# Attention on one Trainium2 core: the statistics of the next batch's first norm taken at the end of a round instead of in the first half of the following one

## What is computed

```python
x = x + 0.5 * _L0_ffn_ref(_layernorm(x), router_w, w1, w2, bias)
x = x + _L0_attn_ref(_layernorm(x), w_qkv, w_gated, w_proj, gn_weight, gn_bias)
x = x + 0.5 * _L0_ffn_ref(_layernorm(x), router_w, w1, w2, bias)

def _layernorm(x, axis=-1, eps=1e-05):
    m = jnp.mean(x, axis=axis, keepdims=True)
    v = jnp.var(x, axis=axis, keepdims=True)
    return (x - m) / jnp.sqrt(v + eps)
```

## Time and profile before

| | |
|---|---|
| median of three runs | 2312.23 us |
| time of the profiled execution | 2312.59 us |
| its span, first to last instruction | 2310.8 us |
| outside the span | 1.8 us |
| busy: TensorE, VectorE, ScalarE, GpSimd | 2170.1, 1358.5, 1003.8, 1171.7 us |
| attention stage | about 905 to 1560 us |
| rounds 0 to 7 begin at (`mask(8b, 0)` on VectorE) | 931.55, 988.41, 1055.31, 1125.64, 1201.15, 1271.39, 1342.39, 1417.02 us |

### The profile page before, as it was taken

How to read it: one execution, slowest core, us unless ns; L and a number is a source line. 1 busy time by engine, 2 the same in 40 slices (tenths; PEclk the granted TensorE clock), 3 DMA queues, 4 the chain that set the end, 5 groups by cost and what they waited for, 6 DMA issues and landing times.

```text
span 2310.8 us, 57931 instructions
## 1 busy us (share of the span) xinstructions
PE 2170.1 (94%) x22549; PEld 1907.2 (83%) x22549; DVE 1358.5 (59%) x3312; ACT 1003.8 (43%) x2149; POOL 1171.7 (51%) x911
## 2 busy tenths in 40 slices
PE   7869999999999997999999999849999999999998
PEld 6759999999999987777777777638999999999997
DVE  7755555555555552578778877645555555555553
ACT  4434434343434342446555555434344444444442
POOL 5755777735354533223344453454777654444443
PEclk9999999999999998999999999869999999999999
DMA  9523444434343424102211121123444443434432
GB/s 365 211 81 68 101 93 99 99 87 98 82 104 81 105 55 119 39 21 76 76 40 59 59 77 75 60 81 94 100 92 102 90 101 86 100 87 99 89 80 32
DMA packets 138440, 211.52 MB, mean 92 GB/s; under 512 B 34092, under 2 KB 114544, under 8 KB 132080
## 3 DMA queue, kind: packets, MB, share of 16 engines
q0 software_dynamic: 57344, 69.21, 17.9%
q1 hardware_dynamic: 80912, 139.72, 17.5%
HBM read 138.13 MB, written 72.88 MB: 91 GB/s over the span
## 4 chain that ended last, share of the span: by engine, by line
PE 52%; DVE 4%; issue 2%; ACT 1%; another core or an unknown queue 0%; POOL 0%; DMA 0%; POOLq 0%; DVEq 0%; ACTq 0%
PE bank L675 16%; PE bank L657 15%; PE bank L768 10%; PE bank L856 3%; PE bank L889 1%; PE bank L824 1%; PE bank L644 1%; PE bank L839 1%; PE bank L874 1%; PE bank L928 1%; PE bank L786 1%; DVE aw L1829 0%; DVE rt L1817 0%; DVE xnl L1803 0%
## 5 line engine op out<-in xcount | busy, mean ns | idle before, releaser
L1167 ACT ACTIVATE h<-bank 128x512 f32<-128x512 f32 x512 | 306.1, 598 | 850.9 <-PE bank L657 740.0
L1738 DVE CAST hh<-h 128x512 fp32r<-128x512 f32 x512 | 241.2, 471 | 692.6 <-ACT h L1167 578.8
L675 PE MATMUL bank<-w2h,hh 128*128 128x256 f32 x2048 | 579.1, 283 | 3.1 <-ACT yb L1185 3.1
L675 PE MATMUL bank<-w2h,hl 128*128 128x256 f32 x2048 | 573.7, 280 | 0.0
L675 PE MATMUL bank<-w2l,hh 128*128 128x256 f32 x2048 | 573.7, 280 | 0.0
L675 PEld LDWEIGHTS bank<-w2h,hh 128*128 128x128 f32 x2048 | 385.1, 188 | 45.4 <-ACT yb L1185 3.6
L675 PEld LDWEIGHTS bank<-w2h,hl 128*128 128x128 f32 x2048 | 384.8, 188 | 41.5
L675 PEld LDWEIGHTS bank<-w2l,hh 128*128 128x128 f32 x2048 | 385.2, 188 | 39.4
L657 PE MATMUL bank<-xh,w1h 128*128 128x512 f32 x1024 | 405.1, 396 | 2.0 <-issue 1.7
L657 PE MATMUL bank<-xh,w1l 128*128 128x512 f32 x1024 | 404.3, 395 | 0.0
L657 PE MATMUL bank<-xl,w1h 128*128 128x512 f32 x1024 | 404.1, 395 | 0.0
(11 more groups left out here) (215 smaller groups left out, 3305.0 us busy)
## 6 DMA issues: line engine op xcount, KB each, us to landing
stg<-in_L_ffn_w SPq DMA_DIRECT2D x64, 1024.0 KB
xb<-acc SPq DMA_DIRECT2D x9, 1024.0 KB
xa<-in_L_attn_x SPq DMA_DIRECT2D x8, 1024.0 KB, 14.4
xn_rows<-xa SPq DMA_DIRECT2D x8, 1024.0 KB
xn_rows<-xn_r SPq DMA_DIRECT2D x8, 1024.0 KB
xr<-acc SPq DMA_DIRECT2D x7, 1024.0 KB
out_rows<-xr SPq DMA_DIRECT2D x7, 1024.0 KB
slot_table<-pay,idx POOLq DMA_INDIRECT x256
```

Source lines behind the costliest of these rows:

```text
L675: product = pe.matmul(tile_sum(j, t, end), a[:, fj, t * P:(t + 1) * P], c[:, fj, :], start=(fj == 0 and i == 0 and (end or t % 2 == 0)), s ...
L1167: act.activation(h32[fj % 2][:], bank[fj % 2][:], ACT.Gelu_apprx_tanh).then_inc(f.gelu, 1)
L1738: dve.tensor_copy(hh[:, fj, :], h32[fj % 2][:]).then_inc(f.hh, 1)
```

## The change

Only the order of VectorE's list in the attention stage changes; no instruction is added or removed. In round b, the four calls `front_stats(b + 1, 0..3)` leave the first half. At the end of round b, behind `front_low(b + 1, 3)`, there are four calls `front_stats(b + 2, 0..3)`, among and behind `channel_stats(n + 6)` and `carry(n + 8, 1)`. Batch 0's statistics are taken ahead of round -1. Batch 1's are now taken at the end of round -1 and batch 7's at the end of round 5.

```diff
                 mask(n, 0)
                 channel_stats(n - 1)
-                front_stats(b + 1, 0)
                 channels(b - 1)
...
                 about_head(b - 1)
-                front_stats(b + 1, 1)
                 head_variance(b - 1)
                 mask(n + 1, 0)
                 carry(n + 1, 1)
-                front_stats(b + 1, 2)
                 rotate(n + 3)
...
                 affine(b - 1)
-                front_stats(b + 1, 3)
                 residual_choices(b - 2)
...
                 front_low(b + 1, 3)
+                front_stats(b + 2, 0)
                 channel_stats(n + 6)
+                front_stats(b + 2, 1)
                 carry(n + 8, 1)
+                front_stats(b + 2, 2)
+                front_stats(b + 2, 3)
...
             start_residual()
+            for j in range(NT // 2):
+                front_stats(0, j)
             for b in range(-1, B):
                 sequence(b)
```

## The result

Timed in turns with the kernel before, the changed kernel takes 2318.02 us (median of 19 runs, 2313.07 to 2323.24) against 2312.87 us (19 runs, 2306.39 to 2317.22): 5.15 us more, a ratio of 1.0027 with a 95% interval of 1.0019 to 1.0036. The interval lies clear of 1. The forecast was 2316.1 us, that is +3.9 us or 0.17%, and the range 2311.5 to 2320.0. The measured time lies inside the range. The difference is larger than the forecast's +3.9 us, and close to the +5.35 us of rival 1 with one stretch of low clock (2317.6 us; two would make 2319.0).

A forecast was written before the change was run, and what follows sets the result against it. TensorE, nearly full, was taken to bound the kernel, so VectorE edits count only where TensorE waits. Terms 0 + 0 + 1.9 + 2.0 = +3.9 us on 2312.2 gave 2316.1 us, range 2311.5 to 2320.0.

The forecast's parts named there:

- rival 1: TensorE's clock falls behind new idle time in rounds 0 and 1; 1.45 us per stretch, 2317.6 us with one; chance 0.27.
- First half of the rounds: Removing 2.64 us of VectorE statistics from the first half of rounds 0 to 6 gains 0.
- line 1558 was to wait about 0.1 us or less: Sign in rounds 2 to 6: VectorE's first routing step hardly waits for TensorE's turned logits.
- End of rounds 1 to 5: Added statistics fit VectorE's free 2.24 us; mask at most 0.40 us late, covered by projection products; cost 0.
- the idle time that the prediction called gone: Sign at the meetings of rounds 1 to 5: VectorE no longer idles ahead of the mask, and TensorE doesn't wait.
- End of round -1: Four statistics pairs delay `mask(0, 0)` by 2.64 us, so TensorE's `scores(0, 1)` starts late; cost 1.9 us.
- End of round 0: VectorE has no slack; later masks and line 1888 delay TensorE's `head_variances` in round 1; cost 2.0 us.
- The loads: Statistics at a round's end now need a load issued in the same round; wait costed at 0.
- The clock: The forecast's sum held no cost for a fall of TensorE's clock behind the new waits: 0.
- Rivals 2: The last statistics pair ahead of the routing gains 0.66 us in each of rounds 2 to 6; 2312.8 us; chance 0.14.
- rival 3: Costs at rounds -1 and 0 are made up later, first halves gain; about 2307.6 us or less; chance 0.05.
- rival 4: A load lands late and `front_stats(2, 0)` waits at the end of round 0; 2317.1 us; chance 0.05.

The follow-up runs named there:

- experiments 6 and 7: 6: kernel before without the statistics of batches 3 to 7, ratio 1.0004; 7: kernel before with each round's first statistics pair moved behind `about_head`, ratio 1.0002.
- late_only: Kernel before with statistics moved to the end of a round only for batches 3 to 7; ratio 0.9994.
- batch2_only: Kernel before with only batch 2's statistics moved, to the end of round 0; ratio 1.0009.
- changed_again: The changed kernel unaltered, profiled and timed a second time against the kernel before; ratio 1.0025, 2299.07 us.
- fill_waits: Changed kernel with TensorE's waits ahead of `scores(0, 1)` and round 1's `head_variances` filled by unread transposes; ratio 1.0010 against the kernel before.
- the doubled one: Changed kernel with eight more unread `bn_stats` at the ends of rounds -1 and 0 each; ratios to the kernel before 1.0058 and, repeated, 1.0059.

## Why the prediction was right and where it was short

- **First half of the rounds, taken as 0: right.** No statistics at all for batches 3 to 7 gains nothing (1.0004). For rounds 2 to 6 the reason is the one given, TensorE's turned logits and then GpSimd's step. One detail was wrong: line 1558 was to wait about 0.1 us or less in rounds 2 to 6, and it waits 0.51 us in each, as in round 7. The working had itself said that the freed time turns up there as idle time. The Trainium skill (SBUF — State Buffer, Who interferes with whom) has such steps blocked for a whole GpSimd instruction; the pairs of rows of experiments 6 and 7 agree, with common ends to within 0.1 us.
- **End of rounds 1 to 5, taken as 0: right.** The mask came 0.22 us late in `late_only` (bound 0.40) and nobody waited. In the profile of the changed kernel the mask of round 6 (at 1355.02 us) still stands idle for 0.64 us until TensorE has its scores; TensorE's clock was low just there (0.50 from 1354 on). So the idle time that the prediction called gone was not gone in every round.
- **End of round -1, taken as 1.9 us: right.** 1.87, 1.88 and 1.87 us in three kernels.
- **End of round 0, taken as 2.0 us: somewhat too much.** The net waits were 1.19 us in the profile of after, 1.44 in `batch2_only` and 1.44 in `changed_again`. `scores(8, 1)` waits 0.44 to 0.68 us, and then `head_variances` 1.21 or 1.22, of which 0.46 were there. VectorE's part was right: the first mask is 2.64 us later in its list, and the second follows 2.33 us behind it (forecast 2.25). But the wait is VectorE's lateness against TensorE, and the working took TensorE as on time. Its `scores(8, 0)`, ahead of the projection products, started at these times before and after, and the last line is VectorE's line 1888 after:

```profile
987.68 0.67 PE L856 MATMUL bank<-qm,qkT 32*64 32x128 f32 x16
...
998.81 0.67 PE L856 MATMUL bank<-qm,qkT 32*64 32x128 f32 x16
...
1007.26 0.16 DVE L1888 SCALAR_TENSOR_TENSOR gsm<-gmv,gsm 128x2 f32<-128x2 f32 x1
```

  From the first to line 1888 it is 7.20 us before and 8.45 after: 1.25 us more, where the working had 1.98. TensorE was late itself, since its clock was low just ahead: from `front_pair` (line 786) to `scores(8, 0)` it took 2.02 us before and 2.67, 2.44 and 2.62 in the three profiles. That accounts for most of what is missing. How long the waits are with a full clock ahead of round 1 was not measured.
- **The loads, taken as 0: right.** In the profile of after VectorE waits for `xb` once, for batch 0, and never again in the attention stage.
- **The clock, taken as 0 in the forecast: the term that failed.** The waits give 3.1 to 3.3 us, the median 5.15 and the repeated comparison 0.25%, 5.7 us. The remainder, 2 to 2.5 us, is put down to the clock; it lies between the 3.7 and the 1.2 us that the low time of the two profiles is worth. On the changed kernel itself this wasn't shown by time (`fill_waits` did not decide); on the doubled one it was. Rival 1 named the mechanism and the price of one stretch, 1.45 us, and gave it 0.27. The case against it was that TensorE waits about 1 us in rounds 4 and 7 without a fall. That was true of the `attend` waits there, but it didn't carry over to waits at other places, and of 1.2 us and more. Behind the wait of round 0 the low stretch was also longer than the one of the earlier trace rows, from about 940 to 946 us, so it would cost about twice 1.45.
- The sum as it came out: 1.9 + 1.3 for the waits + 2 to 2.5 for the clock as the remainder = 5.2 to 5.7 us, where the forecast had 1.9 + 2.0 + 0. The forecast's 3.9 us came near in part by luck: 0.6 to 0.8 us too much for the end of round 0 made up for some of the missing clock.

Rivals 2 and 3 (a gain in the first halves) fell with experiment 6, rival 3 also with the result itself, rival 4 (a late load) with the list of waits. What stays open is why the clock falls behind a given wait in one execution and not in the next, and behind waits of one length at one place and not at another.

## What to carry to other kernels

Slack at a place in a hand-written order belongs to a round, not to the place: the end of a round had 2.2 us of it on VectorE in round 5 and none in rounds -1 and 0, where the software pipeline (the overlap of several batches) is still filling. An edit that is the same in every round costs most in the first rounds, so read those first. And a wait put on a TensorE that is otherwise full can have two prices, its length and the clock behind it; where the second counts, compare the wait as it is with the wait filled by idle work. With the longest waits here (4.5 and 3.5 us) the second was about as large as the first: 7.8 of 14.3 us.

## What the runs showed of the hardware that was not expected

- The granted clock fell to 1.2 GHz behind waits of 1.2 us, in the midst of a TensorE that was otherwise full: behind 1.21 or 1.22 us in 3 of 3 profiles, behind 1.87 or 1.88 us in 2 of 3, in or behind 3.47 to 4.50 us in 4 of 4, behind the 0.45 us of `head_variances` in 1 of 6, and where the waits were filled in none. In the six profiles without an added wait it never fell in the first 20 us of round 0. Length alone doesn't decide it: TensorE also waits 0.73 to 1.72 us for GpSimd's `qk` (line 504) shortly before round 0 in all 13 profiles, and within 5 us behind this wait the clock fell in none. The Trainium skill (TensorE: Matmul & The Clock Gate, HAM oscillation) ties the fall to gaps much longer than 1.2 us; the measurement decides.
- Waits of TensorE that no semaphore released stand near the end of round 0 in all 13 profiles, 1.28 to 4.48 us long. Their length varied between executions of one kernel (1.55 against 4.48 us). In them or within 2.5 us behind them the clock fell in 7 of the 13, and the length did not decide it: behind 1.28 us in 3 of 6, behind 1.55, 3.01 and 4.48 us, not behind 1.56, 1.60 and 1.81 us. What these waits are was not followed up. They are no part of the change, and a round's length in one profile is to be read with them in mind.
